# SwitchHead attention: where the value projection and the gates' broadcast stand within a turn

## The reference

```python
def _moe_attn(x, Wq, Wk, Wv, Wo, Wsel_v, Wsel_o):
    q = _rope(jnp.einsum('bsd,hdp->bhsp', x, Wq))
    k = _rope(jnp.einsum('bsd,hdp->bhsp', x, Wk))
    gv = _gate(x, Wsel_v)
    v = jnp.einsum('bsd,bhse,hedp->bhsp', x, gv, Wv)
    att = jax.nn.softmax(jnp.einsum('bhsp,bhtp->bhst', q, k) / np.sqrt(P), axis=-1)
    o = jnp.einsum('bhst,bhtp->bhsp', att, v)
    go = _gate(x, Wsel_o)
    return jnp.einsum('bhsp,bhse,hepd->bsd', o, go, Wo)
```

## Time and profile before

| what | value |
|---|---|
| three runs | 5591.4, 5591.6, 5593.49 us; median 5591.6 us |
| the profiled execution | 5590.29 us, of which the span in the trace is 5588.5 us |
| mean granted clock of TensorE | 0.965 |
| TensorE busy with matmuls | 5011.5 us, 90% |
| VectorE, ScalarE, GpSimd busy | 74%, 43%, 49% |
| the SwitchHead turns lie between | about 1115 and 3930 us of the span |

### The profile page before, as it was taken

One profiled execution on the slowest core, in us unless ns is written; L12 is line 12 of the kernel. 1 busy time (PEld: TensorE's weight loads), 2 busy tenths in 40 slices (PEclk: granted clock), 3 DMA queues, 4 the chain that ended last, 5 costly groups with the idle time before them and its releaser, 6 DMA issues.

```text
span 5588.5 us, 69631 instructions
## 1 busy us (share of the span) xinstructions
PE 5011.5 (90%) x23754; PEld 1998.8 (36%) x23754; DVE 4137.2 (74%) x4637; ACT 2428.0 (43%) x2960; POOL 2726.0 (49%) x1591
## 2 busy tenths in 40 slices
PE   7898998699999999999999999999788888888856
PEld 2333333233333333433334333433333332222225
DVE  5899989777767777677776787675776678788831
ACT  5665555132222323323233222332355656677743
POOL 4887888466654665456654554554211221120015
PEclk8999999899999999999999999999899999999978
DMA  4555555210110101101011111001111111101005
GB/s 149 180 192 178 187 188 194 73 38 23 36 33 23 30 23 44 32 23 31 23 44 24 28 40 34 23 24 38 45 39 34 37 37 18 30 24 24 2 14 176
DMA packets 139099, 340.17 MB, mean 61 GB/s; under 512 B 33403, under 2 KB 50302, under 8 KB 138100
## 3 DMA queue, kind: packets, MB, share of 16 engines
q1 hardware_dynamic: 135752, 329.40, 19.9%
q0 software_dynamic: 3008, 6.32, 0.3%
HBM read 289.59 MB, written 35.04 MB: 58 GB/s over the span
## 4 chain that ended last, share of the span: by engine, by line
PE 39%; issue 7%; DVE 4%; ACT 3%; POOL 1%; SPq 0%; DMA 0%; POOLq 0%; ACTq 0%; DVEq 0%
PE ps L2320 8%; PE ps L1377 4%; PE ps L1404 4%; PE ps L1362 3%; PE ps L2291 3%; PE ps L1349 3%; PE ps L2273 3%; PE ps L1340 3%; ACT n_P L2371 3%; DVE n_MX L2450 1%; PE ps L2723 1%; PE ps L1366 1%; PE ps L2734 1%; PE ps L1333 1%; PE ps L2223 1%
## 5 line engine op out<-in xcount | busy, mean ns | idle before, releaser
L2450 DVE TENSOR_REDUCE n_MX<-ps 128x2 f32<-128x1024 f32 (+6 forms) x1034 | 982.7, 980 | 244.1 <-PE ps L2273 139.5
L1956 POOL TENSOR_TENSOR s_PA<-s_PA,shared 128x1024 f32<-128x1024 f32 x384 | 909.2, 2368 | 318.7 <-ACT shared L1532 290.9
L1532 ACT ACTIVATE shared<-ps 128x1024 f32<-128x1024 f32 x512 | 522.6, 1023 | 1127.1 <-PE ps L1366 1114.9
L2371 ACT ACTIVATE n_P<-ps 128x1024 f32<-128x1024 f32 (+4 forms) x1022 | 825.1, 838 | 421.5 <-PE ps L2291 230.3
L767 POOL TENSOR_TENSOR m_PR<-m_HH,m_CS 128x1024 f32<-128x1024 f32 x256 | 606.2, 2384 | 159.8 <-issue 144.2
L1698 DVE TENSOR_REDUCE s_MX<-ps 128x2 f32<-128x1024 f32 x512 | 592.4, 1200 | 5.0 <-PE ps L1349 4.8
L1690 DVE TENSOR_TENSOR XTB<-ps,s_GVJ 128x1024 f32<-128x1024 f32 x256 | 312.8, 1222 | 358.7 <-PE ps L1340 356.8
L1349 PE MATMUL ps<-s_QF 64*128 64x512 f32 x2048 | 500.9, 606 | 71.2 <-DVE XTB L1690 44.8
L1362 PE MATMUL ps<-s_QF 64*128 64x512 f32 x2048 | 554.1, 617 | 6.9 <-DVE s_MX L1698 4.6
L2320 PE MATMUL ps<-n_P,n_VA 128*32 128x512 f32 (+3 forms) x3584 | 515.7, 575 | 8.9 <-ACT n_P L2371 8.8
L544 PE MATMUL ps<-m_PR,ident 128*128 128x512 f32 x1024 | 507.2, 623 | 10.1 <-DVE m_ZS L736 5.7
(11 more groups left out here) (372 smaller groups left out, 7161.7 us busy)
## 6 DMA issues: line engine op xcount, KB each, us to landing
m_CS<-m_rows_c SPq DMA_DIRECT2D x256, 512.0 KB
m_BS<-m_rows_c SPq DMA_DIRECT2D x80, 512.0 KB
s_WV<-in_s_v SPq DMA_DIRECT2D x32, 512.0 KB, 3.8
s_TA<-XTB SPq DMA_DIRECT2D x256, 64.0 KB, 2.3
s_WO<-in_s_o SPq DMA_DIRECT2D x32, 512.0 KB, 3.9
g_WB<-in_g_wx SPq DMA_DIRECT2D x23, 578.0 KB
n_parts<-n_PT SPq DMA_DIRECT2D x14, 768.0 KB, 3.4
shared<-n_parts SPq DMA_DIRECT2D x144, 64.0 KB
```

The costliest lines, as they stand in the source:

```text
L1532: s.activation(self.P[g % 4], ps, ACT.Exp).then_inc(*r.take(step))
L1956: g.tensor_tensor(PA, PA, P, ALU.add).then_inc(self.add_done, 1)
L2371: ins = s.activation(P[:, at:at + x.shape[1], lo:512], x[:, :, lo:512], ACT.Exp, scale=scale)
L2450: ins = v.tensor_reduce(self.MX[:, q, at:at + x.shape[1], hp, t], x[:, :, 0:width], AX.X, ALU.max)
```

## The change

Two steps change their place in a turn. `v` no longer stands near the end of the turn but between the two `col` and the two `row`; as turn 0 has none now, each value projection comes two `col` steps later in the whole list than it did. `bcast` goes from ahead of `values` to behind it, and ahead of `sums`, `qk` and `onto`. Nothing is added or removed, and no instruction changes.

```diff
@@ -960,17 +960,19 @@
             if d == 3 and m > 8:
                 out.append(("out_weights", b, j))
             out.extend(("col", b, j, i // 8, i % 8) for i in (2 * d, 2 * d + 1))
+            if m > 0:
+                next(vs, None)
             next(rows, None)
             next(rows, None)
-        if due(self.BCAST):
-            h, e = part(self.BCAST)
-            out.append(("bcast", *self.of_half(h), e))
         if 0 < m <= 64 * NB:
             k, d0 = (m - 1) // 8, (m - 1) % 8
             for i in (2 * d0, 2 * d0 + 1):
                 out.append(("values", *self.pair(k), i // 8, i % 8))
                 if i % 8 == 7:
                     out.append(("keep", *self.pair(k), i // 8))
+        if due(self.BCAST):
+            h, e = part(self.BCAST)
+            out.append(("bcast", *self.of_half(h), e))
         h, x = part(self.SUMS)
         if due(self.SUMS) and x == 0:
             out.append(("sums", *self.of_half(h)))
@@ -985,7 +987,6 @@
             next(ahead, None)
         out.extend(self.due)
         self.due.clear()
-        next(vs, None)
         if due(self.SUMS):
             out.append(("recip", *self.of_half(h), x))
```

## The result

The changed kernel takes 5710.65 us (median of 5 runs, 5702.11 to 5711.95) against 5591.4 us of the kernel before on the same chip: a ratio of 1.0214, 95% interval 1.0202 to 1.0225, or 119 us more. The forecast was 5684 us, in a range of 5640 to 5722. The span of the profiled execution went from 5588.5 to 5708.8 us, the mean clock from 0.965 to 0.966.

A forecast was written before the change was run, and what follows sets the result against it. TensorE was taken to bound the kernel, busy 98.5% of the steady stretch. 5590.3 us plus 133 for shape changes minus 41 for saved waits gave 5682, with the median 1.3 higher 5684 us; range 5640 to 5722.

The forecast's parts named there:

- What bounds the kernel: In the steady SwitchHead turns, 1230 to 3887 us, TensorE sets the time: busy 98.5%, with 40 us of waits.
- The price of the changes of shape: On TensorE, switching tile shape costs 1.04 us a turn against 0.53; over 247 turns and those with sums, 133 us.
- The two places that the trace before didn't show: Col to v, taken as 0.21 us (bounds 0.10 and 0.21), and values to bcast, 0.09 us (bounds 0 and 0.19).
- The count of turns: All the new steps were taken to be there in turns 9 to 255, 247 turns, for 124 us.
- the rival with only the later start: Each change of shape costs only the later start, 0.10 us, not the slow first matmul: 5625 us, chance 0.07.
- the rivals without a loss: No change: shape changes cost 0.055 us, 5592 us, chance 0.02. Faster: the new places are free, 5551 us, chance 0.03.
- the gain: TensorE's waits for the gates' product mostly vanish, with clock dips behind them: 41 us saved, ends 20 and 55.
- The rival that the waits stay: Delay on VectorE may run on into the next turn's columns and v; gain 0 instead of 41: 5725 us, chance 0.10.
- the likeliest case: Waits mostly gone and shape changes at full price: 5684 us, own range 5655 to 5710, chance 0.78.
- What was said of the profile: Undisturbed turn 10.3 us, weight loads idling about 0.76 to 0.81 us, steady TensorE waits below 15 us, busy above 98%.
- The sign of being wrong: Rows, columns or v waiting for maxima or OG over some 20 us, or v following columns at 0.22 and 0.43 us.

The follow-up runs named there:

- bcast_split: The kernel before with the broadcast moved between the two value products of a turn: 5646.02 us, ratio 1.01 to the kernel before.
- v_64rows: The changed kernel with the value projection issued as 64 rows, two side by side, half its contraction done twice: 5618.42 us, ratio 1.0055 to the kernel before.

## Why the prediction was right, and which term was off

- **What bounds the kernel** held: the loss lies in TensorE's busy time (123.9 us more between the first and the last column step), at the same mean clock and with the same instructions.
- **The price of the changes of shape**, 133 us, held for a turn in which nothing waits: 0.50 us more, and 0.65 with `sums`. It is shown from three sides: by the turn of 10.29 us; by `bcast_split`, which adds two changes without moving much else (57 us, 62 by the same prices); and by `v_64rows`, which takes two away (92 us, 99 by the same prices). The two places that the trace before didn't show came out as their nearest rows: col to v 0.09 and a first matmul 0.10 slower, values to bcast 0.09. The count of turns was off without effect: only 248 turns have a value projection, so that the last seven pay 0.10 us instead of 0.50, but the turns with `sums` pay 0.15 us for it and not 0.13, and summed by turns the price is still about 132 us.
- **The full price against half of it**: the rival with only the later start would have made `bcast_split` 30 to 50 us and `v_64rows` 50 us; it is out. So are the rivals without a loss.
- **The term that was mis-sized is the gain**, put at 41 us (32 of the waits, 5 of the clock, 4 ahead of 1230 us). By 133 less 119, it was 14. In the steady stretch TensorE's idle time fell by 8.8 us only. Ahead of 1230 us nothing was gained: in the same 168 us TensorE was busy for 3.7 us less than before. Of the 39.2 us of the wait for the gates' product the prediction left some 7, and the broadcast's wait of 6.9 us is of that size. What it put at nothing are the waits behind it: qk, which asks for the slot of the row scores right behind the broadcast (12.8 us), and the row scores, whose exponentials stand on ScalarE behind the max step (8.0 us).
- **The rival that the waits stay** (5725 us) came nearer than the likeliest case: 14 us from the measured 5710.65, which lies 27 us above 5684 and just above the 5710 up to which that case was put. The stated range holds it because it reaches from one rival to near the other, and not because the gain was known. The rival's reason, delay that runs on into later steps, is what the traces show, with qk in place of the columns.
- What was said of the profile came true in part: 10.3 us a turn, loads that idle 0.64 to 0.76 us, a busy share of 98.9%; but 31 us of waits instead of under 15. The sign of being wrong that was named, waits of rows, columns or v for maxima or OG, came to 0.9 us: it looked past qk, which waits for these maxima.

How the 14 us divide can be read in part. Between the first and the last column step idle time fell by 6.0 us. By the clock's records the traces show 0.50 there for 34 us before and for 31 us after, which is worth under 2 us where the prediction counted 5. The other 6 us or so are open: they lie in turns with a wait, whose busy time grew by less than the price of an undisturbed turn. That a wait in front of a changed shape takes up part of its price is possible and not shown.

## What to carry to other kernels

Count the changes of tile shape in a steady loop on TensorE: here each costs 0.1 to 0.2 us, and three more in a turn of 9.8 us cost 124 us of TensorE's time, while its idle time fell by 6. Look for places that free a buffer earlier without a change of shape (v beside the output projection). And when a wait is removed in a tightly shared ring, go through every later step that asks for one of its slots and every engine's queue behind it: the delay that made the wait, here long VectorE work, turned up in other waits each time a step was moved, and became smaller only when VectorE work (the reciprocal) went into time in which VectorE idled.

## What the runs showed that was not expected

Small VectorE operations took as long as a large one on GpSimd beside them. GpSimd and VectorE in the changed kernel, the layer norm's operations on 8 columns:

```profile
2403.45 4.86 POOL L1957 TENSOR_TENSOR s_PA<-s_PA,shared 128x1024 f32<-128x1024 f32 x2
...
2408.45 2.34 POOL L1957 TENSOR_TENSOR s_PA<-s_PA,shared 128x1024 f32<-128x1024 f32 x1
```

```profile
2406.01 2.32 DVE L791 TENSOR_TENSOR ln_small<-ln_small 128x8 f32<-128x8 f32 x1
2408.37 0.17 DVE L793 TENSOR_TENSOR ln_small<-ln_small 128x8 f32<-128x8 f32 x1
2408.57 2.25 DVE L795 TENSOR_SCALAR ln_small<-ln_small 128x8 f32<-128x8 f32 x1
```

The same kind of operation takes 0.17 us or 2.3 us, and the long ones end when GpSimd's instruction ends: 2408.33 beside 2408.31, and 2410.82 beside 2410.79. It precedes the 2.21 us wait of the broadcast at 2415.40.

The same holds for the product of the gates' top two that takes 2.82 us in the earlier trace rows and delays the gates' product there. In the trace of the kernel before, its executions in two forms number 56; the first form (min, median and longest in ns):

```profile
L1627 DVE TENSOR_TENSOR s_TG<-s_TG,s_M x42: 691/693/2821, 1134.6 to 2788.7; 128x512 f32<-128x512 f32 x42
```

In 36 of the 56 no GpSimd instruction runs beside it, and it takes 0.69 us; in the 20 others it takes 0.95 to 2.82 us, and each of these ends 0.55 us after the end of a GpSimd instruction. So much of the long VectorE work behind the waits of this document is itself a wait for GpSimd. That rests on these times alone; no run took GpSimd's work away.
